# Three rows of x per context group, and head 0 scored behind the fourth query product

## The reference

```
n = layernorm(x)
q = fq((n @ Wq + bq) / sqrt(32))       # 16 heads of 32; fq rounds to -127..127 times a step,
k = fq(ctx @ Wk + bk)                  #   one step for each row and head
v = fq(ctx @ Wv + bv)                  # here one step for each column, over all 2048 rows
p = fq_unsigned(softmax(q @ k.T))      # 0..255 times a step, one for each row
x = x + (p @ v) @ Wp + bp
x = x + mixture_of_experts(layernorm(x))   # 8 experts, weights from a gate
```

## Time and profile before

| | us |
|---|---|
| median of 3 runs (lowest, highest) | 726.53 (724.64, 728.48) |
| the profiled execution's own time | 725.01 |
| its span | 723.2 |
| busy TensorE, VectorE, ScalarE, POOL | 618.9, 567.9, 462.1, 402.8 |

### The profile page before, as it was taken

The page is one execution under the profiler, slowest core; times in us unless marked ns, Lnnn a source line. Parts: engine busy times, 40 slices in busy tenths (PEclk is TensorE's granted clock), DMA queues, the critical chain, the costliest instruction groups (busy, mean ns, idle before and its releaser), DMA issues.

```text
span 723.2 us, 15795 instructions
## 1 busy us (share of the span) xinstructions
PE 618.9 (86%) x5307; PEld 328.3 (45%) x5307; DVE 567.9 (79%) x926; ACT 462.1 (64%) x559; POOL 402.8 (56%) x455
## 2 busy tenths in 40 slices
PE   6999999666867777777777688799999999999995
PEld 3444444233434333443434356455555555555543
DVE  4998888999999999999999998783646547465430
ACT  6344459789979989898989898343434334344321
POOL 5255458537587878787877874234334453344503
PEclk9999999999999999999999999899999999999998
DMA  7777857999989999999999999269697787967914
GB/s 254 198 148 176 182 135 145 182 190 194 173 165 198 184 198 193 188 192 189 189 189 185 200 176 170 88 213 212 162 253 161 225 221 176 242 157 225 145 27 58
DMA packets 318516, 129.42 MB, mean 179 GB/s; under 512 B 293508, under 2 KB 293508, under 8 KB 318472
## 3 DMA queue, kind: packets, MB, share of 16 engines
q1 hardware_dynamic: 311296, 112.64, 72.8%
q0 software_dynamic: 7168, 16.26, 11.0%
q10 hardware_dynamic: 8, 0.01, 0.0%
HBM read 44.33 MB, written 12.06 MB: 78 GB/s over the span
## 4 chain that ended last, share of the span: by engine, by line
PE 46%; issue 14%; DVE 11%; POOL 8%; DMA 7%; ACT 7%; SPq 5%; POOLq 1%; another core or an unknown queue 0%; ACTq 0%; DVEq 0%
PE psum L1668 43%; DMA work<-work 7%; ACT work L1065 4%; DVE spare L1400 3%; POOL work L672 3%; DVE spare L1391 2%; SPq L483 2%; SPq L481 2%; POOL exp_bias L678 1%; PE psum L1987 1%; SPq L450 1%; ACT work L967 1%; POOL work L657 1%; POOL bias_hl L636 1%; POOL out_dram L846 1%
## 5 line engine op out<-in xcount | busy, mean ns | idle before, releaser
L1065 ACT ACTIVATE work<-spare,exp_bias 128x2048 uint8<-128x2048 f32 (+1 forms) x127 | 253.2, 1995 | 29.3 <-POOL exp_bias L678 21.8
L1400 DVE TENSOR_SCALAR_CACHE_REDUCE spare<-psum,q_step_now 128x1024 f32<-128x1024 f32 x128 | 162.8, 1279 | 2.7 <-PE psum L1839 2.5
L672 POOL CAST work<-work 128x2048 int16<-128x2048 uint8 x70 | 132.3, 1890 | 39.2 <-DMA work<-work 35.4
L1391 DVE TENSOR_SCALAR_CACHE_REDUCE spare<-psum,q_step_now 128x2048 f32<-128x2048 f32 x64 | 150.6, 2353 | 0.1
L1839 PE MATMUL psum<-keys_region,work 128*128 128x512 f16 x256 | 73.1, 385 | 43.0 <-DVE spare L1400 27.1
L834 POOL DMA_INDIRECT work<-x_rows,slot_tok x32 | 49.8, 1558 | 88.5 <-DVE slot_w L1600 75.1
L1839 PE MATMUL psum<-keys_region,bias_hl 128*128 128x512 f16 x256 | 70.6, 381 | 28.4 <-DVE spare L1400 22.9
L846 POOL DMA_INDIRECT out_dram<-keys_region,slot_tok x32 | 51.7, 1615 | 74.8 <-ACT keys_region L1160 67.8
L1798 PEld LDWEIGHTS psum<-values_region,work 128*128 128x128 f16 x2016 | 65.0, 96 | 36.5 <-POOL work L672 21.6
L1668 PE MATMUL psum<-work,spare 128*128 128x480 f16 (+1 forms) x396 | 80.5, 364 | 0.0
L1798 PE MATMUL psum<-values_region,work 128*128 128x32 f16 x2016 | 70.0, 177 | 10.8 <-POOL work L672 7.0
(11 more groups left out here) (250 smaller groups left out, 1005.4 us busy)
## 6 DMA issues: line engine op xcount, KB each, us to landing
spare<-in_L_ffn_Wd_dram SPq DMA_DIRECT2D x8, 1024.0 KB, 15.5
spare<-in_L_ffn_Wg_dram SPq DMA_DIRECT2D x7, 1024.0 KB
spare<-in_L_ffn_Wu_dram SPq DMA_DIRECT2D x7, 1024.0 KB, 10.3
work<-in_ctx_dram SPq DMA_DIRECT2D x3, 1024.0 KB, 5.8
work<-work SPq DMA_TRANSPOSE x174, 3.7
token_region<-in_L_xattn_Wkv_dram SPq DMA_DIRECT2D x2, 1024.0 KB, 6.1
resid<-in_x_dram SPq DMA_DIRECT2D x2, 1024.0 KB, 8.9
out_dram<-work SPq DMA_DIRECT2D x8, 256.0 KB, 2.6
```

What stands on the lines that cost most here:

```text
L672: nc.gpsimd.tensor_copy(p_T_int[h % 4], pair_bytes[h % 4]).then_inc(unpacked, 1)
L1065: nc.scalar.activation(p_out, scores, ACT.Exp, bias=exp_bias[:, h % 4:h % 4 + 1], scale=-1.0, accum_out=p_sum[:, h:h + 1]).then_inc(exp_do ...
L1391: nc.vector.tensor_scalar(staged[h % 4], psum[:, at:at + 4, :].rearrange("p b k -> p (b k)"), q_step_now[:, h:h + 1], None, ALU.mult, ALU.min,
L1400: nc.vector.tensor_scalar(staged[h % 4][:, 1024 * c:1024 * c + 1024], psum[:, at:at + 2, :].rearrange("p b k -> p (b k)"), q_step_now[:, h ...
```

## The change

Three things are reordered. Tiles of x go three to each of the context groups 1 and 2 (ScalarE: behind V copy 1, and between the high part and the V copy of blocks 2 and 3) and two to group 3, and SP and POOL follow. The scores of head 0 come behind the fourth query product, queries 4 to 6 behind them, query 7 behind head 1's first scores. V is rounded in the order 3, 0, 1, 2, so that head 0's scores can be staged over block 3 early; two of the four casts go to POOL, and three of the four folds of Wp behind the first exponential. The first four heads use the staging buffers in the order 0, 2, 1, 3.

```diff
NB = len(BYTE_HEADS)
+ROUNDED = (3, 0, 1, 2)
+FIRST_STAGED = (0, 2, 1, 3)
 FIRST_HEADS = tuple(range(0, H, 2))
...
+        def stage_home(h, first):
+            return staged[FIRST_STAGED[h] if first and h < 4 else h % 4]
+
...
-            def key_pair(i, group=None):
+            def key_pair(i, group=None, rows=()):
                 for b in range(2):
...
                         transpose_ctx(group, b)
-                if i >= 2:
-                    transpose_x(i - 2)
+                    if rows[b:b + 1]:
+                        transpose_x(rows[b])
+                for j in rows[2:]:
+                    transpose_x(j)
...
                 key_pair(2 * g, g + 1)
+                if g:
+                    transpose_x(3 * g - 3)
                 if g < SG - 2:
...
                     sp.dma_start(wq_raw, A_wq.rearrange("(c p) n -> p c n", p=P)).then_inc(wq_in, 16)
-                key_pair(2 * g + 1)
+                key_pair(2 * g + 1, rows=(3 * g - 2, 3 * g - 1) if g else ())
             key_pair(2 * SG - 2)
+            transpose_x(QT - 2)
             sp.dma_start(wp_raw, A_wp.rearrange("(c p) n -> p c n", p=P)).then_inc(wp_in, 16)
-            key_pair(2 * SG - 1)
+            key_pair(2 * SG - 1, rows=(QT - 1,))
...
-                if i == DK - 1:
-                    sp.wait_ge(v_rounded, DK + 1)
-                else:
-                    sp.wait_ge(v_halved, i + 1)
+                sp.wait_ge(v_halved, ROUNDED.index(i) + 1)
                 passed()
...
-            transpose_x(QT - 2)
-            transpose_queries(0)
-            transpose_x(QT - 1)
-            transpose_queries(1)
+            transpose_queries(0, (0,))
             for b in range(2):
...
             sp.wait_ge(x_biased, QT)
-            transpose_values(0)
-            transpose_values(1)
-            transpose_queries(2)
-            transpose_values(2)
+            transpose_values(ROUNDED[0])
+            transpose_values(ROUNDED[1])
+            transpose_queries(0, (1,))
+            transpose_values(ROUNDED[2])
+            transpose_values(ROUNDED[3])
+            transpose_queries(1)
...
                     if first and h == 0:
-                        transpose_values(DK - 1)
-                    if first and h in (3, 4):
-                        transpose_queries(DK - 1, range(h - 3, h - 2))
+                        transpose_queries(2)
+                    if first and h < 2:
+                        transpose_queries(DK - 1, (h,))
                     if h == 8 and i < QT - 1 or i == 1 and h == 14:
...
-            def keys_low(j):
-                for b in range(2):
+            def keys_low(j, parities=range(2)):
+                for b in parities:
                     pool.wait_ge(k_hi, 2 * j + b + 1)
...
             pool.wait_ge(small_in, 64)
-            with pool.Fori(2, QT) as j:
-                keys_low(j)
-                x_low(j - 2)
+            with pool.Fori(1, SG - 1) as g:
+                keys_low(2 * g)
+                x_low(3 * g - 3)
+                for b in range(2):
+                    keys_low(2 * g + 1, (b,))
+                    x_low(3 * g - 2 + b)
+            keys_low(KT // 2 - 2)
             x_low(QT - 2)
+            keys_low(KT // 2 - 1, (0,))
             x_low(QT - 1)
+            keys_low(KT // 2 - 1, (1,))
             pool.wait_ge(x_biased, QT)
...
+            def halve_values(n):
+                pool.wait_ge(v_rounded, n + 1)
+                pool.wait_ge(v_halved, n)
+                nc.gpsimd.tensor_copy(v_T_int[:, ROUNDED[n], :], v_i16[:, ROUNDED[n], :]).then_inc(v_halved, 1)
+
             pool.wait_ge(wq_ready, 1)
-            pool.wait_ge(qT_in[0], 16)
+            pool.wait_ge(k_cut_ready[1], KT // 2)
             clear_queries(own, 0)
+            pool.wait_ge(qT_in[0], 16)
             queries_now(0, 0)
+            halve_values(2)
+            halve_values(3)
             own.base, own.n = own.base + own.n, 0
...
+            def rows_of_x(j):
+                normalise_x(j)
+                x_high(j)
+
             def key_group(g, following, first=False):
...
                     key_high(t)
+                    if t >= 2 and not first and (following or t == 2):
+                        rows_of_x(3 * g - 4 + t)
                     act.wait_ge(v_full, 4 * g + t + 1)
...
                                          bias=bv_col[:, t:t + 1], scale=1.0 / WS).then_inc(v_out[b], 1)
-                    if b and not first:
-                        normalise_x(2 * g + t // 2 - 2)
-                        x_high(2 * g + t // 2 - 2)
+                    if t == 1 and not first:
+                        rows_of_x(3 * g - 3)
                     if t == 0 and following:
...
             key_group(SG - 1, False)
-            normalise_x(QT - 2)
-            def round_values(i):
+            def round_values(n):
+                i = ROUNDED[n]
                 nc.scalar.activation(v_i16[:, i, :], v_T[:, i, :], ACT.Copy, scale=v_rstep[:, i:i + 1]).then_inc(v_rounded, 1)
+
+            def fold_projection(i):
                 nc.scalar.activation(wp_hl[:, 0, i, :], wp_raw[:, i, :], ACT.Copy, scale=v_fold[:, i:i + 1]).then_inc(wp_hi, 1)
-            def cut_queries(i):
-                act.wait_ge(q_out, i + 1)
-                for b in range(2):
-                    if i == DK - 1 and b:
-                        act.wait_ge(q_out, DK + 1)
+            def cut_queries(i, parities=range(2)):
+                for b in parities:
+                    if i % (DK - 1):
+                        act.wait_ge(q_out, i + 2)
+                    else:
+                        act.wait_ge(q_out, i + i // 2 + b + 1)
                     act.wait_ge(qT_in[b], 16 * i)
...
             act.wait_ge(v_scaled, 2)
-            act.wait_ge(wp_in, 16)
             round_values(0)
-            x_high(QT - 2)
+            cut_queries(0, (0,))
             round_values(1)
-            normalise_x(QT - 1)
-            cut_queries(0)
-            x_high(QT - 1)
-            round_values(2)
-            cut_queries(1)
+            cut_queries(0, (1,))
             for n in range(2):
                 copy_steps(0, n)
+            round_values(2)
             round_values(3)
-            cut_queries(2)
-            act.wait_ge(v_rounded, DK)
-            nc.scalar.activation(v_T_int[:, DK - 1, :], v_i16[:, DK - 1, :], ACT.Copy).then_inc(v_rounded, 1)
+            act.wait_ge(wp_in, 16)
+            fold_projection(0)
+            cut_queries(1)
...
                     if first and h == 1:
-                        cut_queries(DK - 1)
+                        for c in range(1, DK):
+                            fold_projection(c)
+                        cut_queries(2)
+                    if first and 1 <= h < 3:
+                        cut_queries(DK - 1, (h - 1,))
+                    if first and h < DK:
+                        act.wait_ge(v_halved, ROUNDED.index(h) + 1)
                     if first:
...
                         act.wait_ge(unpacked, unpacked_by(i, 9))
-                    scores = staged[h % 4] if words else staged[h % 4].rearrange("p (c k) -> p c k", c=2)
+                    scores = stage_home(h, first)
+                    if not words:
+                        scores = scores.rearrange("p (c k) -> p c k", c=2)
                     p_out = p_words[h % 4] if words else p_bytes[h % 4]
...
-            def halve_values(i):
-                dve.wait_ge(v_rounded, i + 1)
+            def halve_values(n):
+                dve.wait_ge(v_rounded, n + 1)
                 dve.sem_inc(front_passed, 1)
-                nc.vector.tensor_copy(v_T_int[:, i, :], v_i16[:, i, :]).then_inc(v_halved, 1)
+                nc.vector.tensor_copy(v_T_int[:, ROUNDED[n], :], v_i16[:, ROUNDED[n], :]).then_inc(v_halved, 1)
-            query_tiles(0, 0, 2)
-            halve_values(0)
-            query_tiles(1, 2, 2)
+            query_tiles(0, 0, 1)
+            query_tiles(1, 1, 1)
             dve.wait_ge(wr_centring, 1)
...
                                            wr_raw[:, :, :], ALU.mult, ALU.add).then_inc(wr_centring, 1)
+            halve_values(0)
             halve_values(1)
-            halve_values(2)
-            query_tiles(2, 4, 2)
-            query_tiles(3, 6, 1)
-            base = head + query_steps * (DK + 1)
+            query_tiles(2, 2, 2)
+            base = head + query_steps * (DK + 2)
...
                     dve.wait_ge(exp_done, H * i + h - 3)
+                if first and h == 0:
+                    dve.wait_ge(v_rounded, 1)
+                if first and h == 1:
+                    dve.wait_ge(v_rounded, DK)
                 if first and h == 3:
                     dve.wait_ge(wp_ready, DK)
+                if first and h == 5:
+                    dve.wait_ge(exp_done, 3)
                 if not first and h % HQ == 0:
...
                 at = h % 4
```

(40 more changed lines are left out.)

## The result

The changed kernel takes 740.87 us (median of 6 runs, 740.41 to 742.65) against 725.67 for the kernel before (6 runs, 722.48 to 728.48): ratio 1.0233, 95% interval 1.0209 to 1.0257. It is slower by some 15 us; 738 had been forecast, in a range of 725 to 744. The profiled execution took 740.67 us for a span of 738.9, against 723.2 before. A few executions fell in a slower state of the chip; medians are of all executions, ratios leave these out.

What follows compares the result with a forecast made beforehand. TensorE sets the pace until the last query product, VectorE from about head 2. v_fold's end at 118.0 plus 24.2 puts head 2 at 142.2 against 130.06, +12.1 us: 738 us forecast, range 725 to 744.

Steps and rivals of the forecast that it cites:

- Part 1: Key stage: x_high waits for the single x_hl buffer, delaying V copies; v_fold's end at 118.0 instead of 105.2.
- The load held row B: SP queue, key stage: row B's transpose behind the 1 MB load lands at T + 26.7 instead of T + 25.65.
- Part 2: Front of attention: from v_fold's end to head 2 takes 24.2 us; the reordering alone gains 2.2 us.
- V + 24.2: Front of attention: VectorE stages head 2 24.2 us after v_fold's end (V), at 142.2 against 130.06.
- V + 14.4: Front of attention: TensorE finishes queries 4 and 5 14.4 us after v_fold's end (V); VectorE waits 2.8 us.
- The clock: TensorE under queries 4 and 5: a fall to the lower clock adds up to 1.6 us, upper bound only.
- The value transposes on SP: SP in the front: issued before exp 0, two more query transposes behind; costed at nothing.
- The gain of 2.2: Front: by its reordering alone, with v_fold's end at 103.7, head 2 at 127.9, 2.2 us earlier than before.
- the 1.5 us that I credited: Key stage, VectorE: POOL's row 6 work ends earlier, so value_maxima to v_fold's end takes 23.8 us, not 25.3.
- Rival A: Key stage: the x waits hide; head 2 moves -2.2 to -0.7 us, 724 to 726; 13 in 100.
- rival C: Key stage: one group only, about half the delay stays, +3.7 to +8 us, 730 to 734; 9 in 100.
- B: Rival: x waits hide and VectorE never waits in the front; -5.0 us, 721.5; 5 in 100.
- the chain of 8.8 us: Front: from v_fold's end, rounding, cut, SP transpose, POOL copies and scores of head 0 take 8.8 us.

Runs made afterwards that it cites:

- keep_clock: Changed kernel plus 14 throwaway products on TensorE in its pause ahead of head 0's scores; 739.03 us (one execution), head 2 at 144.48.
- no_waits_plain_front: Changed kernel with x_hl in three buffers and the rows of x behind the V copies, front untouched; 727.66 us, ratio 1.0064 to the kernel before.
- three_buffers: Changed kernel with x_hl in three buffers, one for each place in a group; 727.73 us, ratio 1.0105 to the kernel before.
- copies_first: Changed kernel, still one x_hl buffer, with ScalarE's rows of x behind the V copies of blocks 2 and 3; 728.46 us, ratio 1.0100 to the kernel before.

## Why the prediction held, and where it was off

**Part 1, the rows of x**, went step by step as written. value_maxima at 66.73 and 94.22 (forecast 66.2 and 94.2); row B landed within 3.6 us of its issue at 89.03, 7.6 behind the load's issue (7.9); v_fold's end at 117.8 (118.0); queries from 110.82 (111 to 112). That 94.22 fits to 0.02 is luck: group 1 was 0.5 late, and group 2 took 27.5 us from value_maxima to value_maxima instead of 28.0. The load held row B for 0.5 us only (3.6 us to landing, 3.1 in the earlier trace rows) where the sum has 1.05. With the changed front throughout, v_fold's end came at 117.8 with one buffer and the rows ahead of the V copies, at 107.5 with the rows behind them, at 106.2 with three buffers, and at 105.3 with both. So the cause is shown: the wait for the single buffer, on an engine that has the V copies queued behind it.

**Part 2, the front**, is the step that failed: "Head 2 is staged at V + 24.2", and with it "the reordering of the front gives 2 us". It took 27.9 us, and the front alone costs about 3 where I had 2 of gain. Up to the POOL copies all held (end at V + 7.7). Query tiles 4 and 5 began at V + 16.2 for V + 14.4, and from there to head 2 it took 11.6 us for 9.8. Three terms were missing or too small, and together they make 3.4 of the 3.7 us:
- The clock. I had the fall as an upper bound of 1.6 us and not in the sum; it was 1.8 at the start of query tiles 4 and 5, by keep_clock. The Trainium skill's rule (TensorE: Matmul & The Clock Gate, Part 1: half clock after idling) had it in, and the trace agrees with it for the pause of 3.26 us: scores of 1.81 us behind it, of 1.02 to 1.03 behind pauses of 1.55 (no_waits_plain_front) and 2.19 us (three_buffers) or none.
- "The value transposes on SP are issued before exp 0, two more query transposes behind it ...: no term." That was wrong: the queries' buffers are freed only by their transposes, and these are queued behind V's. It shows as 0.53 us in the changed kernel, 1.84 in keep_clock, 2.83 in no_waits_plain_front, and nothing once the order on SP is right. Where the clock holds, it is the largest term by far: in no_waits_plain_front 2.8 of the 4.0 us over 24.2.
- Tiny operations of VectorE beside POOL's folds of wp. From the changed kernel's VectorE: pair 4 and 5, a tiny operation of tile 6, its rounding, head 2.

```profile
134.02 1.22 DVE L1349 TENSOR_REDUCE row_scales<-psum 128x32 f32<-128x1024 f32 x1 [3.47 <-PE psum L1713]
...
137.98 0.89 DVE L1350 TENSOR_SCALAR scratch<-row_scales 128x16 f32<-128x16 f32 x1
...
139.79 0.69 DVE L1355 SCALAR_TENSOR_TENSOR work<-psum,row_scales 128x512 int16<-128x512 f32 x1 [0.53 <-ACT work L1004]
...
145.66 2.35 DVE L1427 TENSOR_SCALAR_CACHE_REDUCE spare<-psum,q_step_now 128x2048 f32<-128x2048 f32 x1
```

The one at 137.98 took 0.89 us where the same operation of query tiles 0 to 5 took 0.17 or 0.18; with tile 7's (0.53) that is 1.1 us over. It ended at 138.87, and POOL's fold beside it ended at 138.83. In the key stage such an operation took 1.16, 1.16 and 1.17 us when it began with one of POOL's (at 72.41, 82.54 and 100.39) and 0.17 with POOL idle (97.72, 111.56). That POOL holds it up is argued from such times side by side; no run took POOL's work away.

The gain of 2.2 had a second error. It let v_fold's end come at 103.7 if the x waits hid; with them gone V was 105.1 to 105.5. Of the 1.5 us that I credited for POOL's work being over earlier, 1.3 came (v_step and v_fold took 0.56 and 0.14 in the changed kernel, 0.92 and 1.11 before), but with three rows the end of the key stage came 1.5 later by itself (the last value_maxima at 103.05 in no_waits_plain_front, 101.57 before). The traces show where: value_maxima of group 2 started 0.4 later, and two operations of VectorE behind it, each beside POOL's work on a row of x, took 0.71 and 1.23 us for 0.17 and 0.69 before. What came back at one place was lost at others; that POOL is the cause is argued here too.

The total came out 3 us short of the measured 15, inside the range, because part 1 makes up most of it: part 2 alone had the wrong sign. Rival A and rival C were ruled out by 94.22; B by the chain of 8.8 us, which took 9.7 with the slow scores and 9.0 in no_waits_plain_front.

## What to carry to other kernels

Ask of a wait what stands behind it in the same engine's order, not how long it is: four waits of about 3 us cost 12 us with the V copies behind them and about 2 with the rows last. A single buffer refilled by a DMA has a ring time (here 5 to 6 us with its landing); filling it faster than that stalls whoever fills it. Count a shared DMA queue as an engine: in the front, the first two orders on SP moved the same wait from place to place and the third took it away, and the second delay appeared only when the first had been mended. And take an experiment's aid out again where its cause is gone: the throwaway products saved 1.8 us at one place behind a pause of 3.26 us and cost 1.0 where the pause was 1.55.

## What the runs showed of the hardware

How long a transpose takes behind a 1 MB load on the same queue depended here on how close behind it was issued. Issued 2.4 us behind the load it took 5.5 us to land; 3.8 us behind (row B of group 1 in the changed kernel, issued at 61.14) 4.0 us; 4.0 us behind (89.03) 3.6 us; the medians of single transposes of this size were 3.1 and 3.2. All three landed 7.6 to 7.9 us behind the load's issue, but the last was nearly undisturbed.

TensorE's granted clock fell to 0.50 behind the pause of 3.26 us ahead of head 0's scores, and in copies_first, behind one of 3.36, the same scores took 1.86 us. Behind pauses of 1.55 and 2.19 us at the same place it stayed at 1.00. At other places it fell behind shorter pauses: to a mean of 0.62 behind 2.74 us in the changed kernel's key stage, and to 0.50 from 130 to 132 us in the kernel before, behind 2.41 us.
